# Latent values of two heads in one product, and the projections dealt anew over the windows, in an attention and LoRA kernel

## The reference

```
q  = rope(x @ w_q)   32 heads of 128        k  = rope(x @ w_k), v = x @ w_v   8 heads, each shared by 4 query heads
lk = rope((x @ w_lq) @ w_lk)   32 heads     lv = x @ w_lv                     32 heads
attn = causal_softmax(q k^T / sqrt(128)) v      lat = causal_softmax(q lk^T / sqrt(128)) lv
y = x + attn @ w_o + lat @ w_lo
```

## Time and profile before

| | |
|---|---|
| median of 3 runs | 2166.24 us (2165.63 to 2167.49) |
| profiled execution, time and span | 2170.34 us, 2168.5 us |
| PE busy, PE weight loads busy | 2085.7 us (96%), 1761.5 us (81%) |
| DVE busy | 1582.2 us (73%) |
| ACT busy | 1140.5 us (53%) |
| POOL busy | 883.6 us (41%) |
| granted clock of PE, mean | 0.995 |

### The profile page before, as it was taken

How to read it: one execution, slowest core, us unless ns; L and a number is a source line. 1 busy time by engine, 2 the same in 40 slices (tenths; PEclk the granted TensorE clock), 3 DMA queues, 4 the chain that set the end, 5 groups by cost and what they waited for, 6 DMA issues and landing times.

```text
span 2168.5 us, 37857 instructions
## 1 busy us (share of the span) xinstructions
PE 2085.7 (96%) x11236; PEld 1761.5 (81%) x11236; DVE 1582.2 (73%) x2946; ACT 1140.5 (53%) x2502; POOL 883.6 (41%) x693
## 2 busy tenths in 40 slices
PE   5999999999999999999999999999999999999989
PEld 4888878888788887888788887888878888888877
DVE  6677767777777777777777776777777777777775
ACT  2555545555455554555455554555545555555541
POOL 4334443334534344433533444333453334444311
PEclk9999999999999999999999999999999999999999
DMA  2111111111111111112111111111111111111121
GB/s 95 31 35 41 36 32 41 39 39 44 29 41 27 41 46 31 37 36 41 36 36 34 39 37 32 41 41 37 45 27 41 27 41 46 30 41 31 41 50 39
DMA packets 101898, 84.34 MB, mean 39 GB/s; under 512 B 28200, under 2 KB 73896, under 8 KB 101680
## 3 DMA queue, kind: packets, MB, share of 16 engines
q1 hardware_dynamic: 101680, 81.65, 15.9%
HBM read 79.26 MB, written 2.36 MB: 38 GB/s over the span
## 4 chain that ended last, share of the span: by engine, by line
PE 72%; DVE 14%; issue 8%; POOL 3%; ACT 2%; DVEq 0%; DMA 0%; ACTq 0%; SPq 0%; POOLq 0%
PE scores L415 9%; PE scores L417 8%; PE scores L416 8%; PE bankT L477 8%; PE bankX L415 7%; PE bankX L417 7%; PE bankX L416 7%; PE bankO L415 5%; PE bankO L417 5%; PE bankO L416 5%; DVE rot_half L980 3%; DVE rot_half L979 3%; DVE probs L963 3%; DVE PT_lo L969 2%; POOL KT_lo L1191 1%
## 5 line engine op out<-in xcount | busy, mean ns | idle before, releaser
L703 ACT ACTIVATE PT_hi<-bankT 128x512 fp32r<-128x512 f32 (+2 forms) x640 | 336.2, 532 | 413.7 <-PE bankO L417 353.2
L969 DVE TENSOR_TENSOR PT_lo<-bankT,PT_hi 128x512 fp32r<-128x512 f32 (+2 forms) x640 | 387.4, 609 | 184.5 <-ACT PT_hi L703 179.4
L762 ACT ACTIVATE probs<-probs,nmax 128x128 f32<-128x128 f32 (+7 forms) x512 | 394.8, 773 | 140.1 <-DVE nmax L963 139.7
L963 DVE CUSTOM_DVE_ANT_0 probs<-scores,mask 128x128 f32<-128x128 f32 (+7 forms) x512 | 381.1, 750 | 62.2 <-PE scores L417 59.9
L477 PE MATMUL bankT<-ident,probs 128*128 128x128 f32 x2304 | 379.2, 273 | 5.7 <-DVE PT_lo L969 2.2
L477 PEld LDWEIGHTS bankT<-ident,probs 128*128 128x128 f32 x2304 | 285.3, 140 | 73.1 <-DVE PT_lo L969 18.1
L1197 POOL TENSOR_TENSOR rot<-rot,cos 128x512 f32<-128x512 f32 x144 | 185.3, 1287 | 227.8 <-DVE rot_half L980 227.8
L1191 POOL TENSOR_TENSOR OT_lo<-o_raw,OT_hi 128x512 fp32r<-128x512 f32 x64 | 82.7, 1291 | 403.3 <-ACT OT_hi L703 403.3
L1199 POOL TENSOR_TENSOR rot<-rot,rot_half 128x512 f32<-128x512 f32 x144 | 207.3, 1439 | 11.3
L703 ACT ACTIVATE OT_hi<-o_raw 128x512 fp32r<-128x512 f32 x128 | 80.9, 632 | 187.0 <-DVE o_raw L1034 180.5
L979 DVE TENSOR_TENSOR rot_half<-rot,sin 64x512 f32<-64x512 f32 x144 | 108.7, 755 | 82.9 <-ACT rot L703 79.5
(11 more groups left out here) (241 smaller groups left out, 5213.2 us busy)
## 6 DMA issues: line engine op xcount, KB each, us to landing
inv_b<-inverses SPq DMA_DIRECT2D x128, 256.0 KB, 4.1
stage<-in_L_attn_w_q SPq DMA_DIRECT2D x32, 256.0 KB, 4.7
stage<-in_L_attn_w_lv SPq DMA_DIRECT2D x32, 256.0 KB, 2.8
stage<-in_L_attn_w_o SPq DMA_DIRECT2D x32, 256.0 KB, 4.6
stage<-in_L_attn_w_lo SPq DMA_DIRECT2D x32, 256.0 KB, 2.6
acc<-in_L_attn_hidden_states SPq DMA_DIRECT2D x2, 1024.0 KB, 6.6
stage<-in_L_attn_w_k SPq DMA_DIRECT2D x8, 256.0 KB, 4.8
stage<-in_L_attn_w_v SPq DMA_DIRECT2D x8, 256.0 KB, 4.9
```

Of the source, the lines that this page charges most:

```text
L703: return act.activation(place, src, ACT.Copy)
L762: act.activation(prob_tile(c, t), prob_tile(c, t), ACT.Exp, bias=nmax[:, c, t:t + 1], scale=-1.0, accum_out=rsum[:, c, t:t + 1]).then_inc( ...
L963: dve.tensor_tensor_reduce(place, src, tile_view(mask[:, S - width:S], c), -SCALE, -MASKED, ALU.add, ALU.min, nmax[:, c, t:t + 1]).then_in ...
L969: dve.tensor_tensor(pt_place(1, hh, w, j), bankT[j % 2][:, block_columns(c, j):CH], f32(pt_place(0, hh, w, j)), ALU.subtract).then_inc(pt_ ...
```

## The change

- **Latent values of a pair of heads.** LVT is gone. `latent_values` now takes tokens as the stationary and the weights of two heads (256 columns) as the moving operand, so the values come out with tokens on the partitions. There are four LV pieces for two heads, of two tiles each: 24 matmuls of 256 columns. LV and Wlv are twice as wide. ACT and DVE split each piece directly from the bank; it isn't copied to vT.
- **Pieces over windows.** Even heads (hh 0, 2) make the LV of the pair: pieces 0 and 1 in window 0, 2 and 3 in window 2. Odd heads make the queries of the next two heads: Q in window 0, Q2 in window 2. LK of the next head is made in window 3 (slots 1 and 4) of each head, no more in window 0. K and V of the next group are made in windows 1 to 3 of hh 3. OUT1 takes slots 0, 3, 5, 7 of window 1; OUT0 slots 3, 5, 7 of window 3 and slot 0 of the following window 0.
- **Score tiles.** Windows 2 and 3 get the slots of windows 0 and 1.
- **Rotations.** DVE now rotates every Q, K and LK piece in the slot after it, behind the low part of the block. POOL's and ACT's orders follow (`rope_high_slot` says at which window and slot ACT makes the high part of a piece). The last two parts of the diff below are DVE's order within a slot and the end of POOL's order within a head.
- **Group 0** is written out with an order of its own (no output tiles in its first head); the loop runs over groups 1 to 6.

```diff
-TILE_SLOTS = [[0, 1, 1, 2], [1, 2, 4, 6], [0, 0, 1, 1], [3, 4, 5, 6]]
+TILE_SLOTS = [[0, 1, 1, 2], [1, 2, 4, 6], [0, 1, 1, 2], [1, 2, 4, 6]]
...
-    if w == 0:
-        return {0: ("LK", 0), 1: ("LK", 1), 3: ("LV", 0)}
+    if w == 0:
+        if alone(v, hh):
+            return {0: ("LK_HERE", 0), 1: ("LV", 0), 2: ("LV", 1)}
+        ahead = {1: ("LV", 0), 2: ("LV", 1)} if even else {} if final(v, hh) else {1: ("Q", 0), 2: ("Q", 1)}
+        return {0: ("OUT0", 3), **ahead}
     if w == 1:
-        return {0: ("LV", 1), 1: ("OUT1", 0), 2: ("OUT1", 1), 3: ("LVT", 0), 5: ("LVT", 1), 6: ("OUT1", 2),
-                7: ("OUT1", 3)}
+        if alone(v, hh):
+            return {0: ("LK_HERE", 1), 2: ("Q", 0), 5: ("Q", 1)}
+        keys = {2: ("K", 0), 4: ("K", 1)} if ends else {}
+        return {0: ("OUT1", 0), 3: ("OUT1", 1), 5: ("OUT1", 2), 7: ("OUT1", 3), **keys}
     if w == 2:
-        ahead = {0: ("K", 0), 1: ("K", 1), 2: ("V", 0)} if next_group else {}
-        return {**ahead, 3: ("Q", 0)} if more else {}
-    ahead = {0: ("Q", 1)} if more else {}
-    if next_group:
-        ahead.update({1: ("V", 1), 2: ("VT", 0), 3: ("VT", 1)})
-    slots = (4, 5, 6, 7) if hh == GROUP - 1 else (2, 4, 5, 7)
-    return {**ahead, **{s: ("OUT0", n) for n, s in enumerate(slots)}}
+        ahead = {1: ("LV", 2), 2: ("LV", 3)} if even else {} if final(v, hh) else {1: ("Q2", 0), 2: ("Q2", 1)}
+        return {**({0: ("V", 0)} if ends else {}), **ahead}
+    if final(v, hh):
+        return {3: ("OUT0", 0), 5: ("OUT0", 1), 6: ("OUT0", 2), 7: ("OUT0", 3)}
+    values = {0: ("V", 1), 2: ("VT", 0), 6: ("VT", 1)} if ends else {}
+    return {1: ("LK", 0), 3: ("OUT0", 0), 4: ("LK", 1), 5: ("OUT0", 1), 7: ("OUT0", 2), **values}
...
+def rope_high_slot(w, s):
+
+    return {(0, 0): (0, 3), (0, 1): (1, 1), (0, 2): (1, 3), (1, 0): (1, 3), (1, 2): (1, 6), (1, 4): (2, 0),
+            (1, 5): (2, 0), (2, 1): (3, 0), (2, 2): (3, 2), (3, 1): (3, 5), (3, 4): (3, 7)}[w, s]
...
+            def latent_values(n, bank):
+                for i in range(2):
+                    place = banksX[bank][:, i * LV_PAIR:(i + 1) * LV_PAIR]
+                    rows = slice((2 * n + i) * P, (2 * n + i + 1) * P)
+                    for k in range(ND):
+                        mm = mm3(place, both(xnT, ALL, k, rows), both(Wlv, ALL, k, ALL), k == 0, k == ND - 1)
                 return mm
...
-                        if s in here and here[s][0] not in ("LK", "K"):
-                            piece(g, hh, w, s, *here[s], piece_bank(hh, w, s, more))
+                        if s in here and here[s][0] not in ROPE:
+                            piece(g, hh, w, s, *here[s])
                         if s + 2 < BLOCKS[w]:
                             block_lo(g, hh, w, s + 2)
...
-                        if here.get(s - 1, ("", 0))[0] in ("LK", "K"):
-                            piece(g, hh, w, s - 1, *here[s - 1], piece_bank(hh, w, s - 1, more))
+                        if here.get(s - 1, ("", 0))[0] in ROPE:
+                            piece(g, hh, w, s - 1, *here[s - 1])
...
+                    weights(hh, "Wo", "Wlo")
+                    for n in range(2):
+                        add(hh, "Q2", n)
+                        low(hh, "Q2", n)
+                    add(hh, "LK", 0)
+                    weights(hh, "Wlv0", "Wq")
+                    low(hh, "LK", 0)
+                    add(hh, "LK", 1)
+                    weights(hh, "Wlv1", "Wv")
+                    low(hh, "LK", 1)
+                    out_low(g, hh, 3)
```

More of the change, by code:

```diff
@@ L37, with variant, alone, final @@
 BPH = sum(BLOCKS)
-TILE_SLOTS = [[0, 1, 1, 2], [1, 2, 4, 6], [0, 0, 1, 1], [3, 4, 5, 6]]
-def pieces_of(w, hh, more):
-    next_group = more and hh == GROUP - 1
+TILE_SLOTS = [[0, 1, 1, 2], [1, 2, 4, 6], [0, 1, 1, 2], [1, 2, 4, 6]]
+FIRST, MIDDLE, LAST = "first", "middle", "last"
+def variant(g):
+    return (FIRST if g == 0 else LAST if g == KVH - 1 else MIDDLE) if isinstance(g, int) else MIDDLE
+def alone(v, hh):
+    return v == FIRST and hh == 0
+def final(v, hh):
+    return v == LAST and hh == GROUP - 1
@@ L67, in number_pieces, with numbered @@
+def numbered(v):
+    pieces, frees, ropes, values, loads = {}, {}, {}, {}, {}
     for hh in range(GROUP):
+        for name in weights_of(v, hh).values():
+            loads[hh, name] = len(loads)
         for w in range(NW):
[L69 to L78 removed]
@@ new lines, in numbered, with total, group_start @@
+    return {"piece": pieces, "free": frees, "rope": ropes, "value": values, "load": loads}
+NUMBERS = {v: numbered(v) for v in (FIRST, MIDDLE, LAST)}
+AHEAD = {"piece": 10, "free": 6, "rope": 4, "value": 4, "load": 7}
+ROPES_BEFORE = AHEAD["rope"]
+LV_PAIR = 2 * HD
+def total(what, v):
+    return len(NUMBERS[v][what])
+def group_start(what, g):
+    if isinstance(g, int) and g == 0:
+        return AHEAD[what]
+    return g * total(what, MIDDLE) + (AHEAD[what] + total(what, FIRST) - total(what, MIDDLE))
@@ L181, in attn_ffn_kernel @@
         f32 = lambda ap: ap.bitcast(F32)
+        Wlv_half = [[h[:, :, k * HD:(k + 1) * HD] for h in Wlv] for k in range(2)]
+        Wlq = Wlv_half[0]
         def block_no(g, hh, w, j):
@@ L212, in bank_x_taken @@
-        def bank_x_taken(eng, g, hh, w, s, last):
-            bank = piece_bank(hh, w, s, not (last and hh == GROUP - 1))
-            ahead = [(h2, w2, s2, name) for h2, w2, more in windows(g, last) for s2, name in
-                     sorted(pieces_of(w2, h2, more).items())
-                     if (h2, w2, s2) < (hh, w, s) and piece_bank(h2, w2, s2, more) == bank]
-            if bank and not (ahead and ahead[-1][:2] == (hh, w)):
-                eng.wait_ge(row_maxed, tiles_made(g, hh, w))
-                return
-            if not ahead:
-                eng.wait_ge(x_free, g * FREES_PER_GROUP + FREES_BEFORE)
-                return
-            h2, w2, s2, (name, n) = ahead[-1]
-            if name in ROPE:
-                eng.wait_ge(rope_raw, rope_no(g, h2, name, n) + 1)
+            return number("free", g, hh, w, s) + 1
@@ L253, in last_block, with windows @@
             return block_no(g, hh, w, BLOCKS[w] - 1)
-        def windows(g, last):
+        def windows(g):
             for hh in range(GROUP):
                 for w in range(NW):
-                    yield hh, w, not (last and hh == GROUP - 1)
+                    yield hh, w, not final(variant(g), hh)
         def ring_slot(hh, w, j):
```

512 lines of the change are left out of this document (288 added, 224 removed).

## The result

The changed kernel takes 2338.14 us (median of 4 runs, 2334.93 to 2339.46), the kernel before 2166.86 (4 runs, 2165.63 to 2170.92): 1.0785 times as long, interval 1.0766 to 1.0803. The forecast had 57 us more, the runs show 171. The side was right, the size far too small, and the time lies outside the range. Two steps of the prediction failed. It priced a rotation that meets POOL too low: it takes 2.5 to 3.0 us where the forecast had 1.4 to 2.4. And it had no term for TensorE's clock.

A forecast was written before the change was run, and what follows sets the result against it. PE was taken as the bound, busy 96% of the span. Savings of 91 us and costs of 149 gave net +58 on the profiled 2170.3, so 2228; forecast 2224 us, 2.7% slower, range 2185 to 2265.

The forecast's parts named there:

- What goes: PE saves LVT pieces (-27.8 us), vT waits (-28.0), first head's output tiles (-5.5) and smaller waits (-30): 91 in all.
- -30 for smaller waits: PE's waits for row maximum, QT_lo, the turn, weight loads and hh 3's banks shrink: -30 us, bounds 10 to 40.
- Columns: Latent values keep their columns in twice as many matmuls, 256 columns each, starting 0.1175 us apart: +3.0 us.
- rival of the weight loads: Weight loads set the pace of the 256-column runs: +111 us on the forecast, 2335 us; chance 0.03.
- Window 1 to 2: PE's work there, 2.21 us, falls 0.78 short of the 2.99 from transposes to first product, in 25 heads: +19.5.
- Window 2 to 3, even heads: PE has 1.66 us of work against 2.99 from transposes to first product; lack of 1.33, 16 times: +21.3 us.
- Turns behind a rotation: Rotation delays block 0's low part: window 0 to 1, odd heads, 1.2 us each, +19.2; window 2 to 3, hh 1, 2.6, +20.8.
- Window 3 to 0: LK1's late rotation delays the last exponential, then its high part delays block 0: +65 us, bounds 40 to 85.
- The branch of the loop: Group 0 written out saves one loop jump, about 1.9 us, taken as within the error.
- K in window 1 of hh 3: K rotated in window 1 of hh 3 delays Q2 behind V's cover; costed at nothing.
- the turns stay covered: Rival: DVE's spare time hides the window changes, only half their sum or less is paid; 2078 to 2148 us; chance 0.15.
- POOL becomes the bound of windows 0 and 3: Rival: each rotation meets POOL's ordered work, so every turn with one costs 3 us or more; 2285 us; chance 0.12.

The follow-up runs named there:

- e6: Changed kernel, but DVE rotates the slot 2 piece of first-half windows behind the low part of the next block 1; 2267.95 us, 1.0445.
- e7: Changed kernel, but POOL sums LK1 before it makes the low part of LK0; 2287.74 us, 1.0537.
- e11: Changed kernel with e7, slot 4 pieces rotated behind the row maximum, LK1's high part behind those of blocks 0 and 1; 2238.31 us, 1.0325.
- after: The changed kernel itself, against the kernel before; 2338.14 us, 1.0785.
- e10: Changed kernel with e6, e7, LK1's high part later, window 2 tiles in slots 0, 0, 1, 2, and K, LV2, LV3 moved; 2186.38 us, 1.0080.
- e12: e10 with K back in slots 2 and 4, slot 4 rotations behind the row maximum, slot 2 rotations in the next window's slot 0; 2139.70 us, 0.9871.
- b1: Kernel before, with only Q1 moved from slot 0 to slot 1 of window 3 in hh 0 to 2; 2250.54 us, 1.0388.
- e1: Changed kernel with LK1 moved from slot 4 to slot 2 of window 3, changing places with VT0 in hh 3; 2366.31 us, 1.0898.
- e3: Changed kernel with the score tiles of window 2 in slots 0, 0, 1, 1; 2336.60 us, 1.0762.

## Why the forecast had the side right and the size wrong

The mechanism of the loss was right: turns that no work of PE covers, and rotations that stand ahead of what PE needs. e6, e7 and e11 show it by taking 70, 50 and 49 us away with order alone. Two steps failed. The first is the price of a turn or a row maximum behind a rotation. The forecast let POOL hold a rotation once and for part of an instruction, so that it takes 2.4 us at most. In the turns of the traces POOL holds both halves, and it takes 3.0; in window 3 it takes 2.5 in even heads, where one half waits for most of an instruction, and 2.76 in odd ones, where both are held. The second is the clock, which had no term. Both meet in the turns behind a rotation of windows 0 to 1 and 2 to 3: forecast 40 us, measured some 70 of waits and, with 17 falls, some 29 of clock.

Point by point; the measured values are PE's waits from start to start, summed over a place.

- **What goes.** Right for what it names. No LVT, no wait of PE for vT at the latent values; the work of PE fell by 28 us where -27.8 - 5.5 + 3.0 = -30 were forecast. The -30 for smaller waits was not separated.
- **Columns.** Right in kind, a little too cheap: 24 matmuls of 256 columns in a row start 0.120 us apart and not 0.1175, which makes the term +7 instead of +3. Here in the timeline of after:

```profile
1039.22 0.28 PE L510 MATMUL bankX<-Wlv_hi,xnT_lo 128*128 128x256 f32 x1
1039.34 0.28 PE L511 MATMUL bankX<-Wlv_lo,xnT_hi 128*128 128x256 f32 x1
```

  The rival of the weight loads, with 0.19, falls.
- **Window 1 to 2.** Right: 21.9 for 19.5, 0.87 a turn for 0.78.
- **Window 2 to 3, even heads.** Right: 23.1 for 21.3, 1.44 for 1.33; e10 and e12 confirm it by filling the turn.
- **Turns behind a rotation.** The step that failed most. The mechanism right, the size wrong: 35 for 19.2 in window 0 to 1 (2.2 a turn for 1.2) and 29.5 for 20.8 in hh 1 (3.7 for 2.6, of which 0.5 is the clock), and 8 in hh 3, where I had V1 cover it. The range had the rotation at 1.4 to 2.4. It took 3.0, since both its halves were held. The falls behind these turns come on top. e6 took out 2.2 a turn and 61 us of half clock.
- **Window 3 to 0.** The largest term: about 77 for 65. I let the rotation begin with POOL free until 1.3 and be held once. In the trace POOL is already at work when it begins, so the first half is held, in hh 1 and 3 the second too, and the rotation ends 3.7 to 4.0 us after OUT0 and not 2.6 to 3.1. The wait for the exponential is then 1.8 to 2.05, not 0.8, and an even head loses 2.7 by the table (19.7 for 17.0) where I took 2.2 and gave 2.8 as the upper bound. e7 and e11 take the 2.7 away in two parts: 1.1 by clearing POOL, 1.6 by the order on DVE and ACT. In hh 3 the wait is 1.76 for a forecast of 1.75, which is luck, as it is another wait than the one I added up: the exponential alone, and the turn behind it lies mostly in the loop's branch. The chain of two waits in series was right; its price had the rotation end 0.6 to 0.9 us too early.
- **The branch of the loop.** I had counted one loop jump less, 1.9 us, and not asked what a late PE does to those that stay. They cost 15.8 us for 9.7, and a fall of 6.8 us each, some 16 more.
- **K in window 1 of hh 3, costed at nothing.** Wrong: 9 us. The rotation of K1 stands ahead of the last row maximum of window 1, just as LK1's does in window 3, and PE waits 1.2 for the exponential in seven heads. I had named V's cover of the turn and not asked what stood behind the rotation in its own slot. The same windows have a fall each, worth 11 us, but it begins behind the turn 0 to 1, and e6 removed all seven with K1's rotation left where it was.
- **The clock: no term at all.** Some 45 us of the 171, priced by b1 at 1.6 us for each 3.4. The earlier trace rows and the mean clock of 0.995 gave no warning, because PE had no wait of over 1.9 us within the heads before. Of the 107 us by which the profiled time exceeds the forecast's 2228, the falls account for some 45 and longer waits for the rest. The values above hold little of these 45, since most falls run on behind the wait. With them the points add up to some 110 for the 107, which proves little, since the -30 for smaller waits was not separated.
- **Group 0.** The first two windows of its hh 0 have some 4 us more waiting than before (6.1 in after and 5.1 in e12 for 1.4). What makes it so was not studied.

Of the rivals, "the turns stay covered" fell at once. "POOL becomes the bound of windows 0 and 3" was nearest: it had each rotation meeting POOL and gave 2285. I gave it 0.12, arguing from the average of 1.116. The average was over the old order, in which few rotations met POOL; the change moved the rotations to where POOL is busy. But POOL is no bound by its load (busy 37%): e11, which contains e7, took 100 us away with all its work in place. It holds up others by order.

Two expectations of experiments went the same way, e1 and e3: each removed the wait that it aimed at, and PE met new ones of 0.8 to 1.2 us on the same path. The waits of this kernel have to be taken together, by the order on all engines.

## What to carry to other kernels

A change that moves work between stages keeps the load and changes who meets whom: price a moved instruction by its dearest row beside the neighbour that it will have, not by the mean of where it stood. For every slot, write down what stands behind the moved instruction on its engine, since a rotation of 1.4 us ahead of a row maximum cost the bound engine 1.6 us a window, 2.7 with POOL's order against it, and none behind it. An order that makes the bound engine late also bares what its queue had hidden, here the loop's branch. And if the forecast puts waits of over 2 us in a loop of TensorE that had none, add a term for its clock.
